# Shared block first and routing steps in later slots in the first layer's experts, four banks for up products in the second layer's

## What is computed

```python
x = x + 0.5 * L0_ffn(layernorm(x))
x = x + L0_attn(layernorm(x))
x = x + 0.5 * L0_ffn(layernorm(x))
x = x + 0.5 * L1_ffn(layernorm(x))
x = x + L1_attn(layernorm(x))
x = x + 0.5 * L1_ffn(layernorm(x))

def L0_ffn(x):                                   # 32 routed experts of width 64, top 8, and a shared block of width 64
    aff = sigmoid(x @ Wr + br)
    top_v, top_i = top_k(aff, 8)
    w = zeros.at[top_i].set(top_v / (sum(top_v) + 1e-9))
    shared = (silu(x @ Wg_s + bg_s) * (x @ Wu_s + bu_s)) @ Wd_s + bd_s
    down = (silu(x @ Wg + bg) * (x @ Wu + bu)) @ Wd + bd      # for every expert
    return shared + sum_e w[e] * down[e]

def L1_ffn(x):                                   # 8 experts of width 512, top 2
    r = softmax(mask of the two largest scores of x @ Wr + br)
    return sum_e r[e] * (relu(x @ W1[e] + b1[e]) @ W2[e] + b2[e])
```

## Time and profile before

| | |
|---|---|
| median of 3 runs | 2291.22 us |
| profiled execution, its time / span of its instructions | 2292.7 us / 2291.0 us |
| mean granted TensorE clock | 0.961 |
| TensorE busy | 2094.4 us, 91% |
| VectorE busy | 1694.6 us, 74% |
| ScalarE busy | 1207.0 us, 53% |
| GpSimd busy | 921.4 us, 40% |

### The profile page before, as it was taken

How to read it: one execution, slowest core, us unless ns; L and a number is a source line. 1 busy time by engine, 2 the same in 40 slices (tenths; PEclk the granted TensorE clock), 3 DMA queues, 4 the chain that set the end, 5 groups by cost and what they waited for, 6 DMA issues and landing times.

```text
span 2291.0 us, 45750 instructions
## 1 busy us (share of the span) xinstructions
PE 2094.4 (91%) x10800; PEld 1487.4 (65%) x10800; DVE 1694.6 (74%) x3458; ACT 1207.0 (53%) x1873; POOL 921.4 (40%) x904
## 2 busy tenths in 40 slices
PE   2999899999999889999999999998999898999999
PEld 1777677666666667777777777773333337777777
DVE  4666666777777566667668888886777777888887
ACT  3565565455555566566544444445555554444444
POOL 1555555232323355556534444441121214444444
PEclk9999999999999999999999999999988889999999
DMA  4232234233322223333301111122322201111112
GB/s 158 91 101 97 99 100 141 63 85 101 100 82 83 81 88 111 112 102 115 109 28 43 41 42 45 41 77 90 111 82 88 95 29 38 42 42 41 41 38 73
DMA packets 120751, 180.41 MB, mean 79 GB/s; under 512 B 33664, under 2 KB 38112, under 8 KB 120544
## 3 DMA queue, kind: packets, MB, share of 16 engines
q1 hardware_dynamic: 120672, 179.46, 25.6%
HBM read 148.20 MB, written 31.20 MB: 78 GB/s over the span
## 4 chain that ended last, share of the span: by engine, by line
PE 58%; issue 16%; DVE 12%; POOL 10%; ACT 2%; DMA 1%; DVEq 1%; SPq 1%; POOLq 0%; ACTq 0%
PE pair L381 11%; PE pair L383 11%; PE pair L382 11%; POOL h_lo L1264 8%; PE pair L750 3%; PE bank L585 3%; PE pair L585 3%; PE pair L670 3%; PE bank L571 2%; PE pair L692 2%; PE bank L381 1%; DVE h_hi L1037 1%; DVE rmax L1094 1%; PE bank L383 1%; PE bank L382 1%
## 5 line engine op out<-in xcount | busy, mean ns | idle before, releaser
L1270 POOL TENSOR_TENSOR h_lo<-hid,h_hi 128x512 fp32r<-128x512 f32 x256 | 330.3, 1290 | 473.9 <-ACT h_hi L835 473.6
L1264 POOL TENSOR_TENSOR h_lo<-hid,h_hi 128x512 fp32r<-128x512 f32 x256 | 330.0, 1291 | 335.9 <-ACT h_hi L804 335.0
L381 PE MATMUL pair<-xnT_hi,w_hi 128*128 (+1 forms) x1056 | 439.2, 416 | 20.7 <-DVE h_lo L1039 16.9
L383 PE MATMUL pair<-xnT_hi,w_lo 128*128 (+1 forms) x1056 | 423.8, 401 | 0.0
L382 PE MATMUL pair<-xnT_lo,w_hi 128*128 (+1 forms) x1056 | 423.0, 401 | 0.0
L830 ACT ACTIVATE hid<-pair,bias 128x512 f32<-128x512 f32 x256 | 176.3, 689 | 324.8 <-PE pair L383 321.1
L381 PE MATMUL pair<-h_hi,w_hi 128*128 128x512 f32 x784 | 316.6, 404 | 7.1 <-ACT yT L788 3.5
L383 PE MATMUL pair<-h_hi,w_lo 128*128 128x512 f32 x784 | 310.5, 396 | 0.0
L382 PE MATMUL pair<-h_lo,w_hi 128*128 128x512 f32 x784 | 309.7, 395 | 0.0
L1017 DVE SCALAR_TENSOR_TENSOR prod<-pair,bias,wb 128x512 f32<-128x512 f32 x256 | 191.3, 747 | 120.8 <-PE pair L383 104.2
L1037 DVE TENSOR_SCALAR h_hi<-pair,nb 128x512 fp32r<-128x512 f32 x256 | 191.0, 746 | 106.1 <-PE pair L383 105.5
(11 more groups left out here) (173 smaller groups left out, 3368.3 us busy)
## 6 DMA issues: line engine op xcount, KB each, us to landing
wb<-parts_dram SPq DMA_DIRECT2D x512, 128.0 KB, 2.8
wb<-parts_dram SPq DMA_DIRECT2D x128, 256.0 KB, 3.3
parts_dram<-attn_parts SPq DMA_DIRECT2D x96, 256.0 KB, 3.0
attn_q_st<-parts_dram SPq DMA_DIRECT2D x64, 256.0 KB, 2.7
k_one<-parts_dram SPq DMA_DIRECT2D x128, 64.0 KB, 2.3
attn_k_st<-parts_dram SPq DMA_DIRECT2D x32, 256.0 KB, 3.0
stage_w<-in_w_dram SPq DMA_DIRECT2D x32, 130.0 KB, 2.1
stage_w<-in_w_dram SPq DMA_DIRECT2D x6, 512.0 KB, 8.8
```

What stands on the lines that cost most here:

```text
L381: eng.matmul(o, w_hi_, v_hi, start=start, stop=False, **kw)
L383: return eng.matmul(o, w_lo_, v_hi, start=False, stop=stop, **kw)
L1264: eng.tensor_tensor(h_lo[:, p % NH0, :], hid[:, p % NHID, :] if p < NP else hs[:, :], h_hi[:, p % NH0, :].bitcast(F32), ALU.subtract).then ...
L1270: eng.tensor_tensor(h_lo[:, j % NH1, :], hid[:, j // 2 % NHID, :], h_hi[:, j % NH1, :].bitcast(F32), ALU.subtract).then_inc(lo1p_ready, 1)
```

## The change

The shared block runs in slot 0 and the pairs in slots 1 to 16 (`unit_of` maps a slot to its weights). The steps of the layer norm and the router move to later slots by the tables. The weights' transposes are copied by ScalarE straight into partitions 64 to 95 of `hs`, the store to DRAM reads them there, and `shared_weights`, its DMA and its semaphore go. In ffn1 the up products use four banks (0, 1, 2, 4) instead of three, and `wT` and `wT_out` move from slot 26 to 27.

```diff
+NU = 4
 PREP = {
-    "ffn0": ((0, 0, 1, 2, 3, 4, 4, 5), (6, 6, 7, 7, 8, 9, 10, 10, 11, 12, 12)),
-    "ffn0 after attn0": ((4, 4, 5, 8, 8, 10, 10, 11), (12, 12, 13, 13, 13, 13, 14, 14, 14, 15, 15)),
+    "ffn0": ((0, 1, 2, 3, 4, 6, 6, 7), (8, 8, 9, 9, 10, 11, 12, 12, 13, 15, 15)),
+    "ffn0 after attn0": ((4, 4, 5, 8, 8, 10, 10, 11), (12, 12, 13, 13, 13, 14, 14, 14, 15, 16, 16)),
...
-    "ffn1": ((4, 5, 6, 8, 9, 12, 12, 14), (16, 16, 18, 18, 19, 20, 21, 23, 24, 26, 26)),
+    "ffn1": ((4, 5, 6, 8, 9, 12, 12, 14), (16, 16, 18, 18, 19, 20, 21, 23, 24, 27, 27)),
...
+        def unit_bank(j):
+            return bank[(0, 1, 2, 4)[j % NU]]
+        def unit_of(k):
+            return NP if k == 0 else k - 1
+        def weight_rows(ch):
+            return (hs, bd_rows) if ch.kind == "ffn0" else (lgT, slice(0, E1))
...
-            products(eng, gate_bank(p)[:, :], w0_hi[:, GATE0 + p, :], w0_lo[:, GATE0 + p, :], xh, xl).then_inc(g_ready, 1)
+            products(eng, gate_bank(p)[:, :], w0_hi[:, GATE0 + unit_of(p), :], w0_lo[:, GATE0 + unit_of(p), :], xh, xl).then_inc(g_ready, 1)
...
-            behind = reader(j, 3, NJ) - 1
+            behind = reader(j, NU, NJ) - 1
             eng.wait_ge(lo1v_ready if behind % 2 else hid1_ready, ROUND + ch.g * (NJ // 2) + behind // 2 + 1)
-            products(eng, bank[j % 3][:, :], w1_hi[:, UP1 + j, :], w1_lo[:, UP1 + j, :],
+            products(eng, unit_bank(j)[:, :], w1_hi[:, UP1 + j, :], w1_lo[:, UP1 + j, :],
...
             if step == "wT_out":
                 eng.wait_ge(wT_ps, ch.gf + 1)
-                eng.activation(lgT[0:ne, :], bank7[0:ne, :], ACT.Copy).then_inc(wT_ready, 1)
+                dst, rows_ = weight_rows(ch)
+                if ch.very_first:
+                    eng.wait_ge(hs_zeroed, 1)
+                elif ch.kind == "ffn0":
+                    eng.wait_ge(lo_ready, ROUND + (ch.g - 1) * NPS + 1)
+                    eng.wait_ge(w_out, 16 * ch.gf)
+                eng.activation(dst[rows_, :], bank7[0:ne, :], ACT.Copy).then_inc(wT_ready, 1)
...
-                if q == NP:
-                    eng.wait_ge(hs_in, 16 * (ch.g + 1))
-                    eng.wait_ge(hs_zeroed, 1)
-                eng.activation(h_hi[:, q % NH0, :], hid[:, q % NHID, :] if q < NP else hs[:, :], ACT.Copy).then_inc(hi_ready, 1)
+                eng.activation(h_hi[:, q % NH0, :], hid[:, unit_of(q) % NHID, :] if q else hs[:, :], ACT.Copy).then_inc(hi_ready, 1)
...
-            if p == NP:
+            i, b = unit_of(p), BU + unit_of(p)
+            if p == 0:
                 eng.wait_ge(silu_ready, base + p + 1)
-                eng.wait_ge(lo_ready, base)
+                eng.wait_ge(lo_ready, base - LAG)
...
-            eng.wait_ge(*weights_in(ch, p))
+            eng.wait_ge(*weights_in(ch, i))
...
                 if ch.kind == "ffn0":
-                    eng.wait_ge(prod_ready, ROUND + ch.g * NPS + i - NWB + 1)
+                    eng.wait_ge(prod_ready, ROUND + ch.g * NPS + i - NWB + 2)
...
-        def shared_weights(eng, ch):
-            eng.wait_ge(lo_ready, ROUND + ch.g * NPS)
-            eng.wait_ge(hs_zeroed, 1)
-            settle(eng)
-            src = weights[bass.ds(ch.gf, 1), 0:E0, :].rearrange("g e s -> (g e) s")
-            eng.dma_start(hs[bd_rows, :], src).then_inc(hs_in, 16)
```

More of the change, by code:

```diff
@@ L279, in build @@
         g_ready, u_ready = sem("g_ready"), sem("u_ready")
-        w_out, wb_in, hs_in, hs_zeroed = sem("w_out"), [sem(f"wb_in{i}") for i in range(NWB)], sem("hs_in"), sem("hs_zeroed")
+        w_out, wb_in, hs_zeroed = sem("w_out"), [sem(f"wb_in{i}") for i in range(NWB)], sem("hs_zeroed")
         bd_hi_done, bd_lo_done = sem("bd_hi_done"), sem("bd_lo_done")
@@ L538, in down0 @@
                 eng.wait_ge(yT_ready, ch.g)
-            ins = products(eng, bank[5][:, :], w0_hi[:, DOWN0 + p, :], w0_lo[:, DOWN0 + p, :],
+            ins = products(eng, bank[5][:, :], w0_hi[:, DOWN0 + unit_of(p), :], w0_lo[:, DOWN0 + unit_of(p), :],
                            h_hi[:, p % NH0, :], h_lo[:, p % NH0, :], start=(p == 0), stop=(p == NPS - 1))
@@ L829, in act_ffn1 @@
                 eng.wait_ge(lo1p_ready, ROUND + ch.g * half + reader(i, NHID, half))
-                eng.activation(hid[:, i % NHID, :], bank[j % 3][:, :], ACT.Relu, bias=bias[:, B1 + j:B1 + j + 1]).then_inc(hid1_ready, 1)
+                eng.activation(hid[:, i % NHID, :], unit_bank(j)[:, :], ACT.Relu, bias=bias[:, B1 + j:B1 + j + 1]).then_inc(hid1_ready, 1)
                 if j == 0 and ch.s == FIRST1 and ch.first:
@@ L1004, in dve_ffn0 @@
             eng.wait_ge(u_ready, ch.g * NPS + p + 1)
-            if p == NP:
+            i, b = unit_of(p), BU + unit_of(p)
+            if p == 0:
                 eng.wait_ge(silu_ready, base + p + 1)
-                eng.wait_ge(lo_ready, base)
+                eng.wait_ge(lo_ready, base - LAG)
                 settle(eng)
-                eng.scalar_tensor_tensor(hs[0:I0, :], bank[2 + p % 2][0:I0, :], bias[0:I0, BU + p:BU + p + 1], gate[0:I0, :],
+                eng.scalar_tensor_tensor(hs[0:I0, :], bank[2 + p % 2][0:I0, :], bias[0:I0, b:b + 1], gate[0:I0, :],
                                          ALU.add, ALU.mult).then_inc(hid_ready, 1)
@@ L1014, in dve_ffn0 @@
             eng.wait_ge(hid_ready, base + reader(p, 2, NPS))
-            eng.wait_ge(*weights_in(ch, p))
+            eng.wait_ge(*weights_in(ch, i))
             settle(eng)
-            eng.scalar_tensor_tensor(prod[:, p % 2, :], bank[2 + p % 2][:, :], bias[:, BU + p:BU + p + 1], wb[:, p % NWB, :],
+            eng.scalar_tensor_tensor(prod[:, p % 2, :], bank[2 + p % 2][:, :], bias[:, b:b + 1], wb[:, i % NWB, :],
                                      ALU.add, ALU.mult).then_inc(prod_ready, 1)
@@ L1020, in dve_ffn0 @@
             eng.wait_ge(silu_ready, base + p + 1)
-            eng.wait_ge(lo_ready, base + (reader(p, NHID, NP) if p >= NHID else reader(p, NHID, NP) - 1))
-            eng.tensor_tensor(hid[:, p % NHID, :], gate_bank(p)[:, :], prod[:, p % 2, :], ALU.mult).then_inc(hid_ready, 1)
+            eng.wait_ge(lo_ready, base + reader(i, NHID, NP) + (1 if i >= NHID else 0))
+            eng.tensor_tensor(hid[:, i % NHID, :], gate_bank(p)[:, :], prod[:, p % 2, :], ALU.mult).then_inc(hid_ready, 1)
         def fold_bias(eng):
@@ L1263, in pool_main @@
                 eng.wait_ge(hi_ready, ch.g * NPS + p + 1)
-                eng.tensor_tensor(h_lo[:, p % NH0, :], hid[:, p % NHID, :] if p < NP else hs[:, :], h_hi[:, p % NH0, :].bitcast(F32),
+                eng.tensor_tensor(h_lo[:, p % NH0, :], hid[:, unit_of(p) % NHID, :] if p else hs[:, :], h_hi[:, p % NH0, :].bitcast(F32),
                                   ALU.subtract).then_inc(lo_ready, 1)
@@ L1325, in store_weights @@
             ne = E0 if ch.kind == "ffn0" else E1
+            src, rows_ = weight_rows(ch)
             eng.wait_ge(wT_ready, ch.gf + 1)
             settle(eng)
-            eng.dma_start(weights[bass.ds(ch.gf, 1), 0:ne, :].rearrange("g e s -> (g e) s"), lgT[0:ne, :]).then_inc(w_out, 16)
+            eng.dma_start(weights[bass.ds(ch.gf, 1), 0:ne, :].rearrange("g e s -> (g e) s"), src[rows_, :]).then_inc(w_out, 16)
         def spread(eng, ch, i):
@@ L1340, in spread @@
             elif before is not None and before.kind == "ffn0":
-                eng.wait_ge(prod_ready, ROUND + before.g * NPS + NP - NWB + i + 1)
+                eng.wait_ge(prod_ready, ROUND + before.g * NPS + NP - NWB + i + 2)
             elif before is not None and before.kind == "ffn1":
```

17 lines of the change are left out of this document (8 added, 9 removed).

## The result

The changed kernel takes 2208.95 us (median of 4 runs, 2206.3 to 2211.17) against 2291.18 us before in the same session: a ratio of 0.9648, 95% interval 0.9633 to 0.9662, so 3.5% less. 2213 us had been forecast. The profiled execution spans 2206.2 us against 2291.0: 84.8 us less, where the prediction had summed up 78.

A forecast was written before the change was run, and what follows sets the result against it. TensorE was taken as held up by a chain of in-order queues, not an engine's load. Gains of 34.4 (turn), 16.3, 17.6, 19.5, 1.4 and 0.6 less 10.7 and 1.0 gave 78 us: 2213 us, range 2196 to 2250.

The forecast's parts named there:

- The in-order chain: Middle ffn0 chunk worked out through the engines' queues: turn waits 0.27 us instead of 2.65, chunk 40.1 us against 44.3.
- The logits' wait: In ffn0, TensorE's wait for `lo` grows to 1.2 us from about 0.5; term of -10.7 us.
- wT in ffn0: TensorE's wait for the router's weights in ffn0 goes, no wait instead of 0.93 us a chunk; 16.3 us gained.
- The clock: Half-speed matmuls after ten of 15 turn waits in ffn0 vanish; 17.6 us gained.
- The DMA's way: ffn0 routing weights land 7.1 us after wT starts, first use at 9.3; cover 2.2 us for VectorE, 4.4 for TensorE.
- ffn1: Fourth bank and wT one slot later gain one slot, 1.4 us, in each of 14 chunks: 19.5 us.
- loss at the handovers: Where a stage ends and down products follow at once, two handovers lose 0.5 us each at most: -1.0 us.
- The moved wait (1): In ffn0 `xn_b` meets `h_lo` of slot 3 (2233 us), or the clock still falls (2231), both 2250; 26%.
- The absent logits' wait (2): In ffn0 VectorE is further ahead than counted, so logits don't wait: 16.8 us better, 2196 us; 8%.
- The useless bank (3): In ffn1 the fourth bank changes nothing; wT's slot alone brings 1.1 us a chunk: 2217 us, within the forecast.
- The late weights (4): Routing weights land 2.6 us late in 13 chunks: 2247 us; slower than now only from 6 us a chunk; 3%.
- A VectorE bound at 44 us (5): VectorE's queue sets a new chunk time of 44 us, so no effect within 0.5%; 3%.

The follow-up runs named there:

- e4: The changed kernel with the layer norm's steps of ffn0 back in their old slots: 2218.82 us, ratio 0.9687.
- e5: The changed kernel with ffn0's router from logits to top_d one slot later, wT still in slot 15: 2200.73 us, ratio 0.9607.
- e3: The kernel before, shared block last, with only the changed kernel's two ffn0 tables: 2243.95 us, ratio 0.9798.
- e8: The changed kernel with ffn0's whole router one slot later, wT too (slot 16): 2192.46 us, ratio 0.9575.
- e9: The changed kernel with the second layer's weights cut in two pieces a third-stage chunk (slots 5, 16) instead of four: 2205.69 us, ratio 0.962.
- e0: The changed kernel itself, run again in a later session: 2203.18 us, ratio 0.9613.
- e2: The changed kernel with three banks for the up products again, wT of ffn1 still in slot 27: 2216.96 us, ratio 0.9681.
- e1: The kernel before with only the ffn1 part, four banks for up products and wT in slot 27: 2258.04 us, ratio 0.9868.

## Why the prediction held, and where it did not

**The in-order chain** was the step on which most rests, and it held in each of its times. Counted from slot 0 (123.2): prod of slot 1 was forecast at T+4.7 and came at 4.9, `rstd` ended at 9.6 (9.6), `xn_a` started at 9.9 (9.9), `xn_b` at 12.7 (12.7), the logits at 19.4 (19.4), a chunk 40.2 us (40.1). The turn was forecast to wait 0.27 us and waits nothing, and not because its tiles came sooner: TensorE comes later, at T+13.5 instead of 13.13. It loses 0.2 us more than forecast before `y_tok` and some 0.15 in slot 5, two waits too short to be listed.

**The logits' wait** was forecast at 1.2 us and is 1.27: 6.6 + 7.5 us in 13 waits (7.2 in the six middle chunks shown above, 0.3 in the last) plus 0.16 each, 16.2 us, against 6.1 before, so -10.1 for a term of -10.7.

**wT in ffn0** waits nothing, as forecast (+16.3), but for the first chunk of the third stage (1.31 us idle against 3.06).

**The clock**: forecast as gone, +17.6, and gone from the chunks: none of the 13 logits' waits is followed by a slow stretch, and PEclk is 1.00 from 60 to 330 us (0.98 up to the 400 us of the prediction's sign, since the stage ends before). This was the boldest term, resting on one kind of wait of 1.34 us. That shorter waits leave the clock up is borne out by e4 (3 falls in 15 at 2.0 us) and e5; why is not shown. Where stages hand over the clock still falls: PEclk is 0.50 from 1089 to 1094 us, as it was 0.59 from 1151 to 1155 before.

**The DMA's way** had cover as forecast: no prod of the first stage waits for `wb`, and e3 and e8, each with one slot less, show waits of 1 and 0.7 us. The expectations of e3 and e8 had called this just covered (7.1 against 7.2 us); it is short by some 0.7 to 1 us, since the way takes 7.6 to 8.1 us and not 7.1 (157.94 to 165.87 in e8). The first term of the forecast's sum was too small: 0.65 us from wT's start to ScalarE's copy. Measured it is 1.4 to 1.6, because a high part, itself held up by its `hid`, stands in ScalarE's queue before the copy:

```profile
119.25 0.63 ACT L820 ACTIVATE h_hi<-hid 128x512 fp32r<-128x512 f32 x1 [1.42 <-DVE hid L1040]
119.91 0.59 ACT L793 ACTIVATE hs<-bank 32x512 f32<-32x512 f32 x1
```

The changed kernel's wT before these rows starts at 118.37; prod of slot 1 comes 9.7 us after it, so the cover held with 2 us to spare.

**ffn1** is the term that was mis-sized: 19.5 forecast, 14 x 2.15 = 30 measured (the sign "48.5 us apart" reads 47.73). The mechanism was as told for the bank (0.51 us left of 1.34, forecast 0.64), but "the weights still let it start at 1344.53" was wrong. They come about 0.77 us sooner, and with the slot's 1.4 that is the 2.16. Half of it is the lock by GpSimd's `h_lo`, which no longer falls on their last operation. In the kernel before it did:

```profile
1343.55 0.93 DVE L980 TENSOR_TENSOR wgt<-wgt,den 128x32 f32<-128x32 f32 x1
```
```profile
1343.15 1.27 POOL L1270 TENSOR_TENSOR h_lo<-hid,h_hi 128x512 fp32r<-128x512 f32 x1 [2.94 <-ACT h_hi L835]
```

The other half goes with the 0.36 us behind the turn, a wait that "Nothing else waits" had overlooked. I had read wT's start in the earlier trace rows as a fixed date, while the 0.93 us just before it depended on what stood beside it. The prediction weighed that same lock for `xn_b` in ffn0 alone, where it did not strike.

**What was missed** is the third stage: 1.04 us a chunk for `h_lo` of slot 14, about 6 us in 6 chunks and 1.84 in the last. The middle chunk of the first stage was worked out and taken for the third too, whose ScalarE and GpSimd also cut four pieces of weights. e9, which leaves none between slots 5 and 16, shows them to be the cause.

Together: 38.4 + 16.3 - 10.1 + 17.6 + 30 - 8.1 = 84.1 of 84.8 us. The two errors, +10.5 in ffn1 and -8 in the third stage, all but cancel, so that 2213 lay nearer to 2209 than its terms deserve: that part is luck.

The 84.1 should not be read as a closed account either. It leaves out the start of the first stage, where the wait for prod fell from 2.4 to 0.9 us (1.4 forecast), and that of the third, where wT waits 1.75 us less (0.6 forecast) and ten slow matmuls behind it, 1.9 us, went too. The other way, the stretch over attn1 (between the turns at 1444.5 and 1833.0) took 388.5 us against 383.3 before, though nothing in that stage was changed; e0 had 384.2. The forecast's 1.0 us of loss at the handovers could not be told from such differences.

**The rivals.** The moved wait (1) happened in its mild form, already in the sum; the lock on `xn_b` and the falling clock did not. The absent logits' wait (2) did not happen; e8 had to move the step to get it. The useless bank (3) is refuted by e2. The late weights (4) did not occur, and even e3 and e8, with a slot less, show them at 0.7 to 2 us, far from the 6 that would make the kernel slower. A VectorE bound at 44 us (5) is refuted by 39.3 us in e8.

## What to carry to other kernels

Where engines run hand-ordered queues, lay the timelines of one period of each beside one another and follow the chain of operations that are late; the date at which each arrives can be worked out to 0.2 us before anything is built, and to 0.4 for the engine whose waits are the shortest. Compare starts, not only listed waits: three waits here were too short to be listed, and one of them was worth 0.36 us a chunk. Moving a consumer later costs nothing as long as something else can run, but what the producer is late by comes up again at the next consumer: move the whole train, keep two slots where one operation must follow another across three engines, and do it again for every stage with other work in it. A duration that is longer than the same operation's elsewhere is not a cost of its own, but a meeting with another engine, and may go or come by a change in quite another place, or move to the operation beside it.

## What the runs showed of the hardware that was not expected

The granted clock fell not after every wait of a given length. After turn waits of 2.6 to 2.7 us it fell in 10 of 13 cases before and in 8 of 13 in e1, after the two of 1.9 us in each never; after 1.8 to 2.1 us (e4) in 3 of 15, after 1.1 to 1.6 us (e5, 14 waits) in none; each fall meant 5 to 12 matmuls 0.43 us apart instead of 0.233, 1.1 to 2.5 us. A 0.65 us shorter wait (e4 against before) thus saved most of the clock's cost beside its own length.

A VectorE operation on 128x32 took 865 ns in the mean in one order of the other engines and 231 ns in another. Of the 0.74 us that it lost beside GpSimd's `h_lo`, 0.36 moved to the VectorE operation that met that `h_lo` instead, and 0.38 us a chunk were gained.
